# Probabilities turned in 32x32 blocks on VectorE and through DRAM instead of on TensorE, with values and output projection two steps behind the scores

## The reference

```
x = x + tanh(g_xattn) * attention(layernorm(x), ctx, ctx, mask)
x = x + tanh(g_ffn)   * experts(layernorm(x))

attention:  q = rope(query @ wq);  k = rope(key @ wk);  v = value @ wv
            attn = softmax(q k^T / sqrt(128) + mask)      (per head, 64 x 64)
            out  = (attn v) @ wo
experts:    e = argmax(x @ route_w^T);  out = top * (x @ A[e]^T) @ Bw[e]^T
```

## Time and profile before

| | us |
|---|---|
| median of 3 runs | 1091.52 |
| lowest, highest run | 1091.41, 1092.50 |
| profiled execution: span from its first to its last instruction | 1089.0 |
| what lies around the span, against the median | 2.5 |
| TensorE busy in the span | 1082.4 (99%) |
| VectorE, ScalarE, GpSimd busy | 874.1, 636.8, 591.9 |
| DRAM traffic | 122.3 MB read, 82.8 MB written |

### The profile page before, as it was taken

How to read it: one execution, slowest core, us unless ns; L and a number is a source line. 1 busy time by engine, 2 the same in 40 slices (tenths; PEclk the granted TensorE clock), 3 DMA queues, 4 the chain that set the end, 5 groups by cost and what they waited for, 6 DMA issues and landing times.

```text
span 1089.0 us, 17107 instructions
## 1 busy us (share of the span) xinstructions
PE 1082.4 (99%) x5640; PEld 919.3 (84%) x5640; DVE 874.1 (80%) x1423; ACT 636.8 (58%) x1112; POOL 591.9 (54%) x518
## 2 busy tenths in 40 slices
PE   9999999999999999999999999999999999999998
PEld 7888888888888888888888888888888888888886
DVE  7876657888888888888887898777777777777887
ACT  7563476586666666666655545555555555555553
POOL 5552379888877777777754433333333333333423
PEclk9999999999999999999999999999999999999999
DMA  7858964496646464646489546553535353543112
GB/s 258 273 210 336 391 220 183 155 379 201 214 155 213 155 213 156 212 156 212 141 300 380 185 136 205 177 187 111 187 110 187 112 184 114 179 116 118 40 39 78
DMA packets 106087, 206.27 MB, mean 189 GB/s; under 512 B 8849, under 2 KB 58641, under 8 KB 100113
## 3 DMA queue, kind: packets, MB, share of 16 engines
q1 hardware_dynamic: 105424, 204.40, 55.2%
q10 hardware_dynamic: 576, 0.79, 0.2%
HBM read 122.31 MB, written 82.84 MB: 188 GB/s over the span
## 4 chain that ended last, share of the span: by engine, by line
PE 97%; DVE 2%; DMA 0%; issue 0%; ACT 0%; DVEq 0%; SPq 0%
PE attn L945 32%; PE proj L877 28%; PE score L894 10%; PE attn L839 8%; PE score L839 4%; PE turned L839 4%; PE attn L930 3%; PE attn L932 3%; PE turned L905 3%; PE proj L811 1%; PE small L983 1%; PE small L1008 1%; PE score L983 0%; DMA near_raw<-in_ctx 0%; DVE o_s L1270 0%; DVE stats L1140 0%
## 5 line engine op out<-in xcount | busy, mean ns | idle before, releaser
L945 PE MATMUL attn<-wo_s,o_s 128*128 128x512 f32 x1524 | 374.7, 395 | 0.2 <-DVE o_s L1270 0.2
L877 PE MATMUL proj<-xB,wq_s 128*128 128x512 f32 x1344 | 332.6, 391 | 0.0
L945 PEld LDWEIGHTS attn<-wo_s,o_s 128*128 128x128 f32 x1524 | 280.9, 188 | 57.0 <-DVE o_s L1270 0.4
L877 PEld LDWEIGHTS proj<-xB,wq_s 128*128 128x128 f32 x1344 | 252.0, 188 | 51.3 <-issue 0.2
L1863 POOL TENSOR_TENSOR rot<-rot,tab 128x512 f32<-128x512 f32 x110 | 162.3, 1475 | 145.2 <-ACT rot L1584 145.0
L1633 ACT ACTIVATE o_s<-attn 128x512 fp32r<-128x512 f32 x127 | 69.3, 595 | 112.2 <-PE attn L932 112.1
L894 PEld LDWEIGHTS score<-k_r,q_r 128*128 128x128 f32 x1024 | 123.9, 191 | 5.5 <-DVE q_r L1180 0.4
L1175 DVE TENSOR_TENSOR q_r<-q_r,tab 128x512 f32<-128x512 f32 x127 | 120.9, 952 | 1.5 <-ACT x_third L1584 1.4
L894 PE MATMUL score<-k_r,q_r 128*128 128x64 f32 x1024 | 121.3, 271 | 0.0
L1605 ACT ACTIVATE copies<-proj 128x512 f32<-128x512 f32 x96 | 57.5, 599 | 78.0 <-PE proj L877 77.8
L1282 DVE SCALAR_TENSOR_TENSOR acc<-attn,gates_t,acc 128x512 f32<-128x512 f32 x127 | 94.8, 747 | 4.1 <-PE attn L945 1.2
(11 more groups left out here) (269 smaller groups left out, 1681.5 us busy)
## 6 DMA issues: line engine op xcount, KB each, us to landing
wq_kept<-wq_s SPq DMA_DIRECT2D x16, 1792.0 KB, 6.3
wq_s<-wq_kept SPq DMA_DIRECT2D x16, 1792.0 KB, 8.2
v_kept<-vst SPq DMA_DIRECT2D x64, 256.0 KB, 4.3
v_s<-v_kept SPq DMA_DIRECT2D x128, 128.0 KB, 5.0
wo_kept<-wo_s SPq DMA_DIRECT2D x32, 512.0 KB, 5.7
wo_s<-wo_kept SPq DMA_DIRECT2D x32, 512.0 KB, 5.2
k_kept<-kst SPq DMA_DIRECT2D x32, 256.0 KB, 2.2
wq_raw<-in_wq SPq DMA_DIRECT2D x16, 512.0 KB, 7.8
```

The lines of the kernel that those rows point to most:

```text
L877: last = e.matmul(dst[:, :], wq_s[:, b % 2, A, s, kt, :], xB[:, B, mv, kt, :], start=(first and kt == 0 and m == 0), stop=(kt == 1 and m = ...
L945: last = e.matmul(out_bank(k, bp)[:, :], o_s[:, s, bp, h, :], wo_s[n % WO_SLOTS][:, m, :], start=(h == 0 and i == 0), stop=(h == GROUP - 1 ...
```

## The change

For the first 60 steps (`k < WIDE`) the four turns on TensorE are gone. `probs_to_quads` on VectorE turns the 128x512 probabilities in 32x32 blocks into `p_quads`, where even and odd blocks lie apart. `pass_probs` on SP stores `p_quads` to DRAM (`p_kept`, 256 KB), waits until it has landed, and loads it as `p_turned`, in two transfers of 128 KB to 32 partitions each. Keys then lie on 64 partitions and all four sequences and four heads in 1024 columns. `prob_high` becomes two copies of 64x1024, `prob_low` one subtraction of 64x1024. `p_low` has the same layout as `p_high`, with zeros on its upper 64 partitions, so both parts are multiplied with `v_s`, in 256 columns each, and `v_both` and its transfer are gone. `p_quads` takes the place of `prob_odd`: until step 60 there is one buffer for probabilities and one for the turned blocks. Steps 60 to 63 still use TensorE.

Values and output projection now follow two steps behind the scores: in step k TensorE does those of step k - 2, VectorE `attn_low`, `add_out` of k - 2 and `prob_low` of k - 1, ScalarE alike. The loop on TensorE starts at k = 2, with the products of step 1 ahead of it. Expert work and the loads and stores of output weights move back by one step with them, `fetch_values` from even to odd steps; `store_wq` and `fetch_wo` stand behind `pass_probs` of their step on SP. Some semaphores are merged (`small_in`, `constants_set`, `raw_high`).

```diff
@@ transfers, on SP @@
+            def pass_probs(k):
+                e.wait_ge(probs_in_quads, k + 1)
+                if k >= 2:
+                    e.wait_ge(probs_in, 32 * (k - 1))
+                e.dma_start(p_kept[k % 2], p_quads[:, :, :]).then_inc(probs_kept, 16)
+                e.wait_ge(probs_kept, 16 * (k + 1))
+                if k:
+                    e.wait_ge(probs_high, highs_before(k))
+                    e.wait_ge(probs_low, lows_before(k))
+                for part in range(2):
+                    e.dma_start(p_turned[part * QUAD:(part + 1) * QUAD, :].rearrange("p (q n) -> p q n", n=QUAD_COLS),
+                                p_kept[k % 2, :, part, :].rearrange("(q p) n -> p q n", p=QUAD)).then_inc(probs_in, 16)
...
-                    if piece == 3:
-                        store_wq(b)
...
-                if k % 2 == 0 and k and k // 2 + 1 < UNITS:
+                if k % 2 == 1 and k > 1 and k // 2 + 1 < UNITS:
                     fetch_values(k // 2 + 1)
-                if k % 4 == 0:
+                if k < WIDE:
+                    pass_probs(k)
+                for b, piece in weights_of(k):
+                    if piece == 3:
+                        store_wq(b)
+                if k % 4 == 1:
                     G = k // 4
@@ values, on TensorE @@
-                    for twin in range(2):
-                        e.matmul(b[:, cols[twin]], v_s[:, u % 2, twin, tiles[bp], :], p_high[:, twin, cols[bp]],
-                                 start=(twin == 0), stop=False, skip_group_check=True)
-                    e.matmul(b[:, :], v_both[:, u % 2, tiles[bp], :], p_low[:, bp].rearrange("p t n -> p (t n)"),
-                             start=False, stop=True, skip_group_check=True).then_inc(values_used, 1)
+                    for i, part in enumerate((p_high, p_low)):
+                        for twin in range(2):
+                            last = e.matmul(b[:, cols[twin]], v_s[:, u % 2, twin, tiles[bp], :], by_sequence(part)[:, 2 * bp + twin],
+                                            start=(i == 0 and twin == 0), stop=(i == 1), skip_group_check=True)
+                    last.then_inc(values_used, 1)
@@ order, on TensorE @@
-            turn_probs(0)
             scores(1)
             for b, i in last:
                 product(b, i)
-            for k in range(1, WIDE):
+            for b, i in products_of(1)[0] + products_of(1)[2]:
+                product(b, i)
+            for k in range(2, WIDE):
                 first, middle, last = products_of(k)
-                if k > 1:
-                    scores(k)
+                scores(k)
                 between(k, 0)
-                times_values(k - 1)
+                times_values(k - 2)
...
-                project_out(k - 1, 0)
+                project_out(k - 2, 0)
                 between(k, 4)
                 for b, i in middle:
                     product(b, i)
-                turn_probs(k)
                 between(k, 5)
-                project_out(k - 1, 1)
+                project_out(k - 2, 1)
@@ VectorE @@
+            def probs_to_quads(k):
+
+                e.wait_ge(normalised, k + 1)
+                if k:
+                    e.wait_ge(probs_kept, 16 * k)
+                else:
+                    e.wait_ge(made, len(JOBS))
+                e.transpose(p_quads[:, :, :].rearrange("p k (i a) -> p k i a", a=QUAD),
+                            prob_of(k)[:, :].rearrange("p (i k b) -> p k i b", k=2, b=QUAD)).then_inc(probs_in_quads, 1)
+
+            def prob_low(k):
...
+                if k < WIDE:
+                    e.wait_ge(probs_high, highs_before(k) + 1)
+                    keys = HALF_ROWS[0]
+                    e.tensor_tensor(by_quad(p_low[keys, :]), p_turned[keys, :].rearrange("p (q i a) -> p q i a", q=P // QUAD, a=QUAD),
+                                    by_quad(p_high[keys, :].bitcast(F32)), ALU.subtract).then_inc(probs_low, 1)
@@ order, on VectorE, step k @@
+                probs_to_quads(k)
                 between(k, 2)
-                add_out(k - 1, 0)
+                if k > 1:
+                    add_out(k - 2, 0)
...
-                if not together:
-                    prob_low(k, 0)
+                prob_low(k - 1)
@@ ScalarE @@
             def prob_high(k):
-                e.wait_ge(probs_turned, k + 1)
                 if k:
                     e.wait_ge(values_used, PAIRS * k)
...
+                if k < WIDE:
+                    e.wait_ge(probs_in, 32 * (k + 1))
+                    for rows in HALF_ROWS:
+                        e.activation(by_quad(p_high[rows, :]),
+                                     p_turned[HALF_ROWS[0], :].rearrange("p (q i a) -> p q i a", q=P // QUAD, a=QUAD),
+                                     ACT.Copy).then_inc(probs_high, 1)
```

More of the change, by code:

```diff
@@ L271, in norms_of @@
 def norms_of(k):
-    return [t for t in range(HALF_TILES) if 29 + t // 2 == k]
+    return [t for t in range(HALF_TILES) if 30 + t // 2 == k]
 NORMS = [x for n in sorted(X_BESIDE) for x in X_PAIRS[X_BESIDE[n]]]
@@ L1698, in _ @@
                 ropes = ropes_of(k)
+                if k % 4 == 3 and k > 2:
+                    for w in weights_of(k)[:1]:
+                        wq_split(*w)
                 between(k, 0)
-                attn_high(k - 1, 0)
-                attn_high(k - 1, 1)
+                for bp in range(PAIRS) if k > 1 else ():
+                    attn_high(k - 2, bp)
                 if k == 1:
```

217 lines of the change are left out of this document (122 added, 95 removed).

## The result

The changed kernel takes 1163.57 us (median of 4 runs, 1161.87 to 1166.96), the one before 1091.47 on the same chip: ratio 1.0662, 95% interval 1.0644 to 1.068. Forecast were 1093.3 us with a range to 1108; the miss is 70 us. The profiled execution took 1163.05 us, its span is 1161.3.

The account below looks back on a forecast made before the run. TensorE, busy 1082.4 of 1089.0 us, was taken as the bound. Span 1089.0 - 28.2 + 1.0 + 3 + 24.0 + 2 = 1090.8 us, plus 2.5 for the median, gave 1093.3 us, range 1083 to 1108.

Parts of the forecast that it names:

- Turns off TensorE, -28.2: TensorE's queue: 60 steps without turns, 0.47 us saved in each, -28.2 us.
- 25.9: Sign of being right: two steps in the middle take about 25.9 us instead of 26.86.
- Values, +1.0: TensorE's values: one 512-column matmul becomes two of 256 per pair of sequences, +1.0 us, between 0 and 7.7.
- VectorE, +3 (0 to 16): Stalls from VectorE's net 0.9 us more work a step: +3 us, between 0 and 16.
- that just fits: First half: VectorE's 12.25 us plus a 0.6 us wait fits in a TensorE step of 12.96 us.
- The start gap, +24.0: TensorE, ready at 222.3 us, stands until 246.3 for step 0's probabilities: +24.0 us, bounds 14 and 28.
- I cost them at nothing: Weight store, output weights and next keys held back by SP: nothing, except 1 to 3 us late at xB reloads.
- The tail: From the scores of step 63 the order stays; one more step of values and projections is moved work: nothing.
- VectorE becomes the bound: Rival: VectorE's added work exceeds some 0.9 us a step, giving 1103 us, 1122 at both upper ends; chance 0.22.
- TensorE restarts slowly: Rival: TensorE runs slowly after the gap, +1.7 us, and again with each later stall, 1095 to 1098; chance 0.08.
- steps in the first half over 13.1 us (then VectorE): Sign of being wrong: first-half steps above 13.1 us would point to VectorE.
- VectorE's wait for scores nearly gone: Sign of being right: VectorE's idle time waiting for scores, 52.6 us in the odd steps before, nearly vanishes.

Follow-up runs that it names:

- lag_only: Changed kernel with every turn back on TensorE, values and projection still two steps behind, no store, loads or block turn: 1110.39 us.
- both_last: Changed kernel with VectorE's subtraction and block turn moved behind the rotated queries, the subtraction also behind the second addition into acc: 1139.45 us.
- psum_low: Changed kernel with the subtraction of steps 0 to 57 split in two of 64x512 reading an idle PSUM bank instead of p_turned: 1142.29 us.
- no_block_turn: Changed kernel without the block turn, unturned probabilities stored from two buffers in turn and loaded in the same shapes: 1136.96 us.
- lag_dma: Changed kernel with turns back on TensorE and no block turn, but lag, 60 stores and 120 loads kept, loaded data unread: 1127.66 us.
- all_ordered: Changed kernel with subtraction and block turn last, step 0's store before residual loads, query sums before step 1's row sum, wo before store: 1125.04 us.

## Why the prediction was wrong, step by step

The span grew by 72.3 us where the sum had 1.8: 18.1 up to mask 3, 44.0 in steps 3 to 29, 3.3 in step 29, 9.5 behind mask 59, and 2.6 back in steps 30 to 59.

**Turns off TensorE, -28.2.** Right per step: two steps of the second half take 13.65 + 12.29 = 25.94 us in the changed kernel where nothing waits, and "25.9" was foretold. But every second such pair has a wait of 0.96 us for a query and takes 27.15, so that four steps take 53.09 us instead of 53.72, and steps 30 to 59 give 2.6 us of the 13.6 that were counted for them. In steps 3 to 29 the gain was idle time at once.

**Values, +1.0.** Right: the low parts' matmuls took 51.1 us in all in lag_only against 50.3.

**VectorE, +3 (0 to 16).** This step failed. The sizes held (0.70 for 0.69, 1.34 for 1.6), and the prediction added them to a busy time and compared the sum with TensorE's step: "that just fits". By that sum it does, 310.43 us of VectorE in 26 steps, 11.9 a step against 12.96. What it left out is where in the step the work stands and what it runs beside. Steps 3 to 29 cost 44.0 us, or 56 against what the turns should have given there (26 x 0.47). Order alone accounts for 26.2 us of that (392.40 to 366.25 in both_last), reading two operands in SBUF beside GpSimd for 22.6 (369.77 in psum_low), the block turn for 18.4 (374.00 in no_block_turn). Each was changed alone; how far they overlap no run shows. Half of the loss in that stretch is TensorE's clock: TensorE waits 27.7 us, and its matmuls take some 28 us more than the 336 that the work of before without turns takes at full rate.

**The start gap, +24.0.** Right in mechanism and to 0.3 us in the moment at which the values begin (246.3 foretold, though its terms add up to 246.1; 246.06 measured). The stations on the way fit too: SyncE issues the loads at 240.4 (240.0 foretold), ScalarE's copy begins at 243.4 (243.5). The gap is 18.9 and not 24, because TensorE came to it late, at 227.2 instead of 222.3: it had waited 2.8 us for a sum of VectorE, and the six products behind took 2.92 us instead of 1.52. Of the 7.4 us that it was to have saved by then 2.6 were left. By mask 3 the loss is 18.1 us.

**SyncE, "I cost them at nothing".** The text named the steps that reload xB as the exception, with 1 to 3 us. It was one stop of 2.79 us in the changed kernel and 5.70 in lag_dma; step 29 takes 3.3 us more than before. The sum left it out.

**The tail, "moved work and not new. Nothing."** Failed: 9.5 us, some 6.4 of them the moved matmuls, and 2.9 more in which TensorE stands (6.9 us behind mask 59 instead of 4.1). Moved work is free only if the place it leaves was as tight as the place it goes to.

**The rivals.** "VectorE becomes the bound" had the right engine and the right side, with 1103 and a worst case of 1122 against 1163.6, because it priced an excess of busy time. "TensorE restarts slowly" had 1.7 us for each stall, and few stalls; in steps 3 to 29 half rate cost some 28 us. Measured, what follows a stall differs: in lag_only a wait of 0.50 us left the scores at 2.00 us (1.89 undisturbed), in the changed kernel one of 1.44 us was followed by twelve products in 4.51 us (2.91), and one of 2.69 us by 8.7 us at a granted clock of 0.61. The windows of the changed kernel around the latter:

```profile
438.98:454.12 15.14, 12.45 (x67) 10.44 (x66) 12.00 (x17) 8.55 (x14) 12.79 (x10) 1.00 0.45 147
454.12:462.83 8.71, 8.71 (x36) 8.07 (x37) 3.37 (x6) 2.35 (x5) 2.42 (x3) 0.61 0.74 287
462.83:471.00 8.17, 8.17 (x38) 6.76 (x37) 8.03 (x12) 5.87 (x9) 4.58 (x5) 1.00 0.10 36
```

That is (1 - 0.61) x 8.71 = 3.4 us on top of 2.69, so these two kinds of stall cost about double. It isn't their length alone: in both_last waits of 1.60 us, longer than 1.44, left no half rate behind. The changed kernel around its wait of 1.44 us, then both_last around one of 1.60:

```profile
424.00:432.00 8.00, 6.56 (x26) 5.24 (x26) 6.12 (x10) 3.13 (x6) 5.56 (x6) 0.79 0.80 328
```
```profile
412.00:428.00 16.00, 14.40 (x76) 12.32 (x75) 14.31 (x19) 9.01 (x15) 13.06 (x12) 1.00 0.73 260
```

What else decides is not shown. The Trainium skill ("TensorE: Matmul & The Clock Gate", What's actually happening) has the two levels, and the traces agree with them: behind the start gap, from 246.06 to 247.91 us, the granted clock is 0.50, and a pair of values takes 0.63 us there and 0.40 at 1.00.

**The sign named for trouble**, "steps in the first half over 13.1 us (then VectorE)", is what happened: 61.4 / 4 = 15.4 us. "VectorE's wait for scores nearly gone" was wrong: it is still 65.9 us in 45 times, since TensorE, late itself, hands over its scores late.

What stays open: with all orders mended (all_ordered) steps 3 to 29 still take 366.65 us, 30 more than the 348.42 of before less 12 for the turns. Of these, 18.6 us are waits of TensorE and the rest half rate. How they split between the reads beside GpSimd and the later p_low is not settled. The new order and the subtraction from PSUM were not run together, nor was a kernel in which xB is fetched ahead of the probabilities, nor one with more filling.

## What to carry to other kernels

Before adding work to an engine that is 80% busy, read off its timeline what stands behind the place where it goes and who waits for that: an operation with slack belongs behind the operands that the bounding engine needs next. Price a short stall of TensorE at its length as the lower bound and at about twice that as the upper (both were seen here), and an operation with two SBUF operands by its duration where GpSimd has begun before it. A software lag moves a step's work from the start to the tail; count it as a cost unless the start was as full as the tail.

## What was not expected of the hardware

Matmuls that compute nothing can make a kernel faster: 104 of them, busy for 27 us, took 6.3 us off. A VectorE instruction that reads one operand from PSUM instead of SBUF was worth 21 us here, at the same place in the order and with no less work. Of what the order alone gave in steps 3 to 29, three quarters were not waiting but TensorE's matmuls at full rate again. And the turn in blocks is no cheaper for its speed (0.70 us for 128x512 in fp32) when the engine that does it is the one on which all the others wait.
